# A fused state-space, attention and mixture-of-experts kernel: text rows are prepared earlier, logits go between other products, expert tiles are loaded sooner, and TensorE is given unread work

## The chip, the cores and the metric

The kernel runs on one core of a Trainium2 chip. The metric is device time of one execution in microseconds (us). Three runs of the kernel before took 2265.6, 2267.47 and 2272.73 us, so the median is 2267.47 us.

## What is computed

Eight sequences of 768 rows of 256 numbers go through three stages (float32 throughout):

```
K = 2.0 * einsum('chn,hnl->chl', C*B, exp(log_dA * arange(256))).real      # 256 image rows a batch
h = concatenate([K, txt], axis=1)                                          # + 512 text rows
q, k, v = layernorm(h) @ Wq, @ Wk, @ Wv          # 16 query heads, 4 key heads, 64 wide; q, k rotated
h = h + softmax(q k^T / 8) v @ Wo
logits = layernorm(h) @ Wr + br                  # 8 experts, the best 2 of each row, softmax of those 2
h = h + sum over the 2 of gate * (relu(x @ W1[e] + b1[e]) @ W2[e] + b2[e])
```

The image rows come from `x` (8, 256, 64, 2), the text rows from `txt` (8, 512, 256). The output is (8, 768, 256).

## The kernel before, in words

The program is three blocks of instructions with a barrier between them. In a block each engine works through its own list and meets the others at semaphores.

`vandermonde` makes the powers of the state-space model on VectorE, multiplies them on TensorE, and stores the image rows of batch 0 in `img_d`. The rows of the other seven batches stay in the tile `kt`, and are stored at the start of the next block.

`attention` works in 32 iterations (8 batches by 4 key heads) of 24 steps. A step is one tile of 128 queries of one head against 768 keys: TensorE makes the scores in two banks of PSUM (L656), VectorE the row maximum (L812), ScalarE the exponential (L725), VectorE a transpose (L818), and TensorE multiplies by the values (L663). Ahead of the first step stands a start that is not overlapped with any step. SyncE loads batch 0 into `a_x` (`load(0)`, L516 and L517). VectorE takes the statistics of its 6 tiles (`stats`, L496 to L504 and `refine`, L485 to L488) and normalises four of them (L850), GpSimd the other two (L781). TensorE transposes them (jobs "n" of the list `FIRST`, L633), projects keys, the queries of group 0 and of group 1 (L642), ScalarE copies each result out (`evacuate`), VectorE rotates keys and queries of group 0 in four calls of `rotate` (L470 to L475), in scratch that lies in `a_probT`, which shares its memory with `kt`. Then SyncE moves the keys and, with 16 DMAs, the queries (L622), and TensorE starts the first scores. Each projected job needs one of four banks, and the list waits on `x_out` (results copied out) for it.

`route` and `experts` stand in the third block. `route` takes 8 batches, of 6 tiles each: TensorE multiplies the attention rows by `Wo` (`project`, L980, 8 matmuls a tile), VectorE adds the residual and normalises. Of the batch before, TensorE transposes after tile 1 (`turn`, L988), makes the logits after tile 2 (`logits`, L996, 12 matmuls on 8 columns), and counts after tile 3 (`counts`, L1003 and L1004). VectorE chooses the experts (`choose`, L1110 to L1125) and the slots (`place`), and GpSimd scatters the rows to `xs_d`, where each expert has a range of slots (L963). When all are placed, `tile_table` makes on VectorE, for each of 103 tiles of 128 slots, its expert and its first slot (L1190 to L1212), and 128 empty rows ("pads") are written behind each expert's last row (L934, L1066).

`experts` takes the 103 tiles one after the other. SyncE loads the rows (`load`, L1258) and W1 of the expert (`load_w1`, L1262) into a ring of 4, TensorE transposes (L1292), multiplies by W1 (`up`, L1302) and by W2 (`down`, L1309), VectorE adds the bias and multiplies by the gate (L1382, L1384), GpSimd adds the rows to the output by an indirect DMA (L1365). Before SyncE's first row load stands a wait for all that was scattered, the pads and the stored residual (`landed`). GpSimd's add of a tile waits for the adds of the tiles two and three before it; where the expert changes it also waits for the tile just before (the value is in `adds_i`). Tiles beyond the last filled one ("spare" tiles) repeat the last filled tile with a gate of zero, and each of them counts as such a change.

## Time and profile before

| what | value |
|---|---|
| median of 3 runs | 2267.47 us |
| profiled execution, its own time | 2265.04 us |
| its span, first to last instruction | 2263.3 us |
| VectorE busy, 1000 to 1575 us (attention) | 556.40 of 575.00 us |
| TensorE busy, 1700 to 1800 us (route) | 100.00 of 100.00 us |
| TensorE busy, 2000 to 2200 us (experts) | 200.00 of 200.00 us |
| mean granted clock of TensorE | 0.959 |

All times of rows are counted from the span's start. Between the span and the time of the same execution lie 1.74 us. The granted clock is TensorE's share of full speed, and it has two levels here, 1.00 (2.4 GHz) and 0.50 (1.2 GHz). A matmul of float32 stands in the trace as two records, so that 8 matmuls read x16; transposes have one record each.

### The profile page before, as it was taken

To read this page: it belongs to the slowest core of one execution; us is meant where nothing else is said; L and a number is where in the kernel's file an instruction comes from. 1 tells how busy PE (TensorE), PEld (TensorE's weight loads), DVE (VectorE), ACT (ScalarE), POOL (GpSimd) and SP (SyncE) were. 2 spreads that over 40 slices of the span, in tenths; PEclk is the share of its full clock that TensorE was granted. 3 is DMA by queue.
4 is the path that set the end of the run, shared out by engine and by line. 5 is a ranking of instruction groups with operands and counts; after the bars stand their busy time and mean duration, and the time that the engine had idled before them with its cause. 6 is when DMAs were issued, how large, how long until landed. Compare 5 with 4: busy or idle time off the path is not lost. (4 is left out here: it accounts for less than half of the span.)

```text
span 2263.3 us, 59177 instructions
## 1 busy us (share of the span) xinstructions
PE 2047.4 (90%) x21098; PEld 1237.6 (55%) x21099; DVE 1770.0 (78%) x3212; ACT 1072.6 (47%) x2463; POOL 879.4 (39%) x833
## 2 busy tenths in 40 slices
PE   0369999999999999999999999997899949999997
PEld 0234444444444444444444445443588839999996
DVE  8769999999999999999999999999144544444443
ACT  2035655655556555655665565555021114444442
POOL 0023454264344542642444436221034443444443
PEclk6689999999999999999999999999899969999998
DMA  2143543634544445435444453453677648898885
GB/s 51 43 107 90 136 118 92 159 106 103 142 113 126 117 107 137 116 108 128 120 120 120 102 133 105 117 131 95 202 258 269 216 136 212 210 212 209 215 210 117
DMA packets 189542, 317.28 MB, mean 140 GB/s; under 512 B 48661, under 2 KB 127121, under 8 KB 189329
## 3 DMA queue, kind: packets, MB, share of 16 engines
q1 hardware_dynamic: 156640, 275.39, 45.1%
q0 software_dynamic: 19440, 25.83, 6.2%
q10 hardware_dynamic: 13248, 13.13, 1.7%
q8 instruction: 144, 2.36, 0.5%
q14 instruction: 70, 0.57, 0.1%
HBM read 214.75 MB, written 92.31 MB: 136 GB/s over the span
## 5 line engine op out<-in xcount | busy, mean ns | idle before, releaser
L725 ACT ACTIVATE a_prob<-ps_s,a_nmax 128x768 f32<-128x768 f32 x768 | 686.3, 898 | 578.9 <-DVE a_nmax L812 578.9
L812 DVE TENSOR_REDUCE a_nmax<-ps_s 128x1 f32<-128x768 f32 x768 | 694.1, 943 | 49.4 <-PE ps_s L656 44.2
L818 DVE STREAM_TRANSPOSE a_probT<-a_prob 128x768 f32<-128x768 f32 x768 | 700.0, 949 | 1.4 <-PE ps_o L663 1.4
L656 PE MATMUL ps_s<-a_kT,a_qT 64*128 64x384 f32 x3072 | 614.7, 514 | 54.7 <-ACT a_prob L725 50.8
L663 PE MATMUL ps_o<-a_probT,a_vrep 32*64 32x384 f32 x12288 | 561.2, 491 | 6.8 <-DVE a_probT L818 5.0
L656 PEld LDWEIGHTS ps_s<-a_kT,a_qT 64*128 64x128 f32 x3072 | 259.7, 186 | 391.5 <-ACT a_prob L725 275.3
L788 POOL TENSOR_TENSOR a_o<-a_o,a_invrow 128x1536 f32<-128x1536 f32 x32 | 110.0, 3437 | 791.0 <-ACT a_o L733 791.0
L663 PEld LDWEIGHTS ps_o<-a_probT,a_vrep 32*64 32x64 f32 x12288 | 243.6, 132 | 293.8 <-issue 129.9
L470 POOL TENSOR_TENSOR a_prod<-a_raw,a_table 128x384 f32<-128x384 f32 x304 | 294.5, 1002 | 29.1 <-DVE a_qp L475 22.1
L1365 POOL DMA_INDIRECT out_dram<-e_y,e_row_i x103 | 160.6, 1559 | 239.9 <-DMA out_dram<-e_y,e_row_i 138.6
L1302 PE MATMUL ps_r<-e_xT,e_w 128*128 128x128 f32 x1648 | 201.8, 276 | 0.0
L1309 PE MATMUL ps_r<-ew,e_hT 128*128 x824 | 194.7, 379 | 0.0
L1302 PEld LDWEIGHTS ps_r<-e_xT,e_w 128*128 128x128 f32 x1648 | 193.3, 193 | 0.1
L1340 ACT ACTIVATE e_hT<-ps_r,e_b_now 128x128 f32<-128x128 f32 x412 | 117.8, 368 | 158.9 <-PE ps_r L1302 100.0
L980 PE MATMUL ps_r<-wo,r_oT 128*128 128x256 f32 x768 | 180.9, 397 | 9.7 <-POOL base L945 9.7
L642 PE MATMUL ps_o<-a_xT,wq 128*128 128x384 f32 x512 | 185.8, 501 | 0.0
L980 PEld LDWEIGHTS ps_r<-wo,r_oT 128*128 128x128 f32 x768 | 151.5, 200 | 32.2 <-POOL base L945 10.4
L1309 PEld LDWEIGHTS ps_r<-ew,e_hT 128*128 128x128 f32 x824 | 148.8, 190 | 16.0
L963 POOL DMA_INDIRECT xs_d<-r_xn,r_idx x96 | 93.8, 977 | 150.1 <-DVE h L1078 119.1
L725 ACT ACTIVATION_READ_ACCUMULATOR a_prob<-ps_s,a_nmax 128x1 f32 x768 | 151.0, 197 | 0.0
L642 PEld LDWEIGHTS ps_o<-a_xT,wq 128*128 128x128 f32 x512 | 91.0, 189 | 88.9 <-issue 25.6
L1382 DVE TENSOR_TENSOR e_y<-ps_r,eb 128x256 f32<-128x256 f32 x103 | 43.7, 424 | 99.9 <-PE ps_r L1309 97.9
(211 smaller groups left out, 1291.5 us busy)
## 6 DMA issues: line engine op xcount, KB each, us to landing
e_w<-in_L_ffn_W_dram SPq DMA_DIRECT2D x103, 512.0 KB, 4.3
a_qT<-q_d SPq DMA_DIRECT2D x124, 384.0 KB, 8.9
a_vrep<-v_d SPq DMA_DIRECT2D x128, 192.0 KB, 3.8
a_invrow<-inv_d SPq DMA_DIRECT2D x64, 384.0 KB, 5.1
oT_d<-a_o SPq DMA_DIRECT2D x32, 768.0 KB, 3.3
r_oT<-oT_d SPq DMA_DIRECT2D x64, 384.0 KB, 8.4
q_d<-a_qp SPq DMA_DIRECT2D x31, 768.0 KB, 3.7
e_x<-xs_d SPq DMA_DIRECT2D x103, 132.0 KB, 3.6
```

Of the source, the lines that this page charges most:

```text
L470: eng.tensor_tensor(scratch[n], a, f, ALU.mult).then_inc(done, 1)
L642: last = pe.matmul(X[:, 0:HALF], w, xn[:, k, HALF * c:HALF * c + HALF], start=(k == 0), stop=(k == KC - 1))
L656: last = pe.matmul(S[:, s % 2, r, 0:HALF], qT[rows, par, 2 * hp + c, P * t:P * t + P], kT[rows, par, :], start=True, stop=True)
L663: last = pe.matmul(O[DH * c:DH * c + DH, q, 0:HALF], vrep[rows, j % NQ, j // NQ, :], keys(par, c, j, rows), start=(j == 0), stop=(j == NJ ...
L725: act.activation(prob[:, s % RING, :].rearrange("p (r k) -> p r k", r=2), S[:, s % 2, :, 0:HALF], ACT.Exp, bias=nmax[:, s % RING:s % RING ...
L812: v.tensor_reduce(nmax[:, s % RING:s % RING + 1], S[:, s % 2, :, 0:HALF], AX.XY, ALU.max, negate=True).then_inc(max_ready, 1)
L818: v.transpose(turned(par, s), prob[:, s % RING, :]).then_inc(t_ready, 1)
L980: last = pe.matmul(A[:, t % 3, 0:D], oT[:, q, c // 2, c % 2, P * t:P * t + P], wo[:, c, :], start=(c == 0), stop=(c == KV * 2 - 1))
L1302: last = pe.matmul(H[:, q, P * f:P * f + P], w1[:, n, c, P * f:P * f + P], xT[:, q, P * c:P * c + P], start=(c == 0), stop=(c == KC - 1))
L1309: last = pe.matmul(Y[:, q, 0:D], hT[:, q, P * c:P * c + P], w2[:, bass.ds(ex, 1), c, :], start=(c == 0), stop=(c == FC - 1))
L1340: last = act.activation(hT[:, q, P * f:P * f + P], H[:, q, P * f:P * f + P], ACT.Relu, bias=b1_now[:, n, f:f + 1], scale=1.0)
L1365: pool.indirect_dma_start(out=acc_d, out_offset=bass.IndirectOffsetOnAxis(ap=row_i[:, n:n + 1], axis=0), in_=y[:, n, :], in_offset=None, c ...
```

## The change

At the start of attention:
- The text rows of batch 0 are loaded and normalised in the first block, with `normalise_rows` on VectorE. The buffers for it are allocated before both blocks. Only the two image tiles are left for the second block, all on VectorE.
- The list `FIRST` begins with the text transposes (8), the keys of tokens 384 to 767, the image transposes (4), then the other keys, and the queries in the same order of halves.
- `rotate` of these works in `a_prod`, and the wait for `rows_stored` stands behind the four calls. Keys are moved by halves.
- Ahead of the first scores TensorE makes 16 matmuls of the identity by `wv`, 256 columns each, into a bank that nobody reads. They wait until the first job of group 1's queries is copied out.

In the routing:
- the 12 logit matmuls stand in pairs behind the last six of the eight matmuls of tile 2, no longer behind all eight.
- TensorE's first product waits no longer for GpSimd's constants; the counts do.

In the experts:
- SyncE waits no longer for all that was scattered before the first loads. For tiles 0 to 7 it reads from a small table (`needs_i`) whether the rows of the first seven batches fill the tile (`placed` 1) or not (`placed` 2); later tiles wait for `placed` 2. W1 is loaded in turn with the rows. The wait for the stored residual moved to GpSimd.
- A spare tile takes expert 7 and the pads behind its last row. The row numbers in the pads lie beyond the output, so that the add leaves them out, and it no longer counts as a change of expert. The table has some steps fewer.

```diff
+AHEAD = 8
@@ vandermonde
+                sp.dma_start(x0[:, IT:TT, :], io["txt"][0].rearrange("(t p) d -> p t d", p=P)).then_inc(x_in, 16)
...
+                v.wait_ge(x_in, 16)
+                normalise_rows(v, Tally(v, text_dve), x0, ln, range(IT, TT)).then_inc(text_ready, 1)
@@ attention
-    FIRST = N_JOBS + K_JOBS + Q_JOBS + Q_JOBS
+    FIRST = [("text", 0, 0), ("text", 1, 0), ("k", 1, 0), ("k", 1, 1), ("image", 0, 0), ("k", 0, 0), ("k", 0, 1),
+             ("q", 1, 0), ("q", 1, 1), ("q", 0, 0), ("q", 0, 1)] + Q_JOBS
@@ attention, sync
-                hold(sp, part["k"], 2 * LINKS)
-                move_k(0, 0)
+                for r in (1, 0):
+                    hold(sp, part["k"], (2 - r) * LINKS)
...
@@ attention, tensor
-                pe.wait_ge(norm_ready, 1)
-                pe.wait_ge(norm_first, 1)
+                pe.wait_ge(text_ready, 1)
...
+                    if n == IMAGE_AT:
+                        pe.wait_ge(norm_ready, 1)
...
-                pe.wait_ge(x_out, FIRST_AT["q1"])
+                pe.wait_ge(x_out, len(FIRST) - NQ + 1)
+                for _ in range(16):
+                    pe.matmul(O[:, len(FIRST) % NQ, 0:D], ident[:], wv[:, 0, 0:D], start=True, stop=True)
@@ attention, vector
-                v.wait_ge(rows_stored, (NB - 1) * 16)
-                flat = probT[:].rearrange("p a b q -> p (a b q)")
-                for job in "kq":
-                    for c in range(2):
-                        rotate(v, job, c, c, [flat[:, HALF * n:HALF * n + HALF] for n in range(4)], FIRST_AT[job] + 2 * c + 2, [])
+                for job, c, number in (("k", 1, 0), ("k", 0, 1), ("q", 1, 0), ("q", 0, 1)):
+                    rotate(v, job, c, number, [prod[:, n, :] for n in range(4)], FIRST.index((job, c, 1)) + 1, [])
+                v.wait_ge(rows_stored, (NB - 1) * 16)
@@ route, gpsimd
+            if isinstance(b, int) and b >= NB - 2:
+                if b == NB - 1:
+                    for r in range(2):
+                        pool.wait_ge(zeroed[r], 16 * (NE // 2))
+                pool.nop().then_inc(placed, 1)
@@ route, tensor
                 last = pe.matmul(A[:, t % 3, 0:D], oT[:, q, c // 2, c % 2, P * t:P * t + P], wo[:, c, :], start=(c == 0), stop=(c == KV * 2 - 1))
+                if beside is not None and c >= KV * 2 - TT:
+                    logits(beside, [c - (KV * 2 - TT)])
...
-        pe.wait_ge(const, 4)
@@ route, vector
+            k.link(v.tensor_scalar(full[:], off[:, 0, 0:1], 1.0 / P, -1.0, ALU.mult, ALU.add))
+            k.link(v.tensor_scalar(needs_i[:], tile_no[:, 0:AHEAD], full[:], 1.0, ALU.is_gt, ALU.add))
@@ tile_table
-    link(v.tensor_scalar(jr[:], j[:], last[:], None, ALU.min))
...
-    link(v.tensor_scalar(ind[:], j[:], last[:], None, ALU.is_gt))
...
+    v.tensor_scalar(src_i[:], start[:], run[:, NE - 1:NE], None, ALU.min).then_inc(rows_ready, 1)
...
-    link(v.tensor_tensor(turn[:, 1:NT], turn[:, 1:NT], ind[:, 1:NT], ALU.max))
@@ experts, sync
         def load(j, n):
+            if isinstance(j, int) and j < AHEAD:
+                needs = sp.value_load(at(needs_i, j), min_val=1, max_val=2)
+                hold(sp, placed, needs)
...
-        for n in range(2):
-            load_w1(n, n)
-        for s, value in landed:
-            sp.wait_ge(s, value)
         for n in range(RING):
             load(n, n)
-        for n in range(2, RING):
             load_w1(n, n)
@@ experts, gpsimd
+        pool.wait_ge(h_stored, 16 * NB)
```

What the change moves is seen in each engine's list of instructions. First TensorE's list at the start of attention, the kernel before (`a_x` holds the normalised rows, `wk` the key weights; the waits are in brackets):

```order
L633 MATMUL ps_o<-ident,a_x 128x128 [waits loaded,a_norm_first,a_norm_ready]
L633 MATMUL ps_o<-ident,a_x 128x128 x11
L642 MATMUL ps_o<-a_xT,wk 128x384 [waits a_x_out]
L642 MATMUL ps_o<-a_xT,wk 128x384
L642 MATMUL ps_o<-a_xT,wk 128x384 [waits a_x_out]
L642 MATMUL ps_o<-a_xT,wk 128x384
```

The same place in the changed kernel:

```order
L663 MATMUL ps_o<-ident,a_x 128x128 [waits loaded,a_text_ready]
L663 MATMUL ps_o<-ident,a_x 128x128 x7
L679 MATMUL ps_o<-a_xT,wk 128x384 [waits a_x_out]
L679 MATMUL ps_o<-a_xT,wk 128x384 x3
L666 MATMUL ps_o<-ident,a_x 128x128 [waits a_x_out,a_norm_ready]
L666 MATMUL ps_o<-ident,a_x 128x128 x3
L679 MATMUL ps_o<-a_xT,wk 128x384 [waits a_x_out]
L679 MATMUL ps_o<-a_xT,wk 128x384
```

The wait for the image's normalisation (`a_norm_ready`) now stands behind eight text transposes and four key matmuls.

Second, TensorE's list of one batch of the routing, the kernel before (`wo` is the output projection, `wr` the router, `r_xT` the transposed rows of the batch before):

```order
L980 MATMUL ps_r<-wo,r_oT 128x256 [waits r_h1_ready]
L980 MATMUL ps_r<-wo,r_oT 128x256 x7
L992 ISA
L996 MATMUL ps_r<-wr,r_xT 128x8 [waits r_mask_ready,r_xT_ready]
L996 MATMUL ps_r<-wr,r_xT 128x8 x11
```

And in the changed kernel:

```order
L1025 MATMUL ps_r<-wo,r_oT 128x256 [waits r_h1_ready]
L1025 MATMUL ps_r<-wo,r_oT 128x256 x2
L1040 ISA
L1044 MATMUL ps_r<-wr,r_xT 128x8 [waits r_mask_ready,r_xT_ready]
L1044 MATMUL ps_r<-wr,r_xT 128x8
L1025 MATMUL ps_r<-wo,r_oT 128x256
L1044 MATMUL ps_r<-wr,r_xT 128x8 x2
L1025 MATMUL ps_r<-wo,r_oT 128x256
L1044 MATMUL ps_r<-wr,r_xT 128x8 x2
```

The number of matmuls is the same; the logits moved into the product of tile 2, and their wait for `r_xT_ready` with them.

Third, SyncE's list at the start of the experts, the kernel before (`exp_i` and `src_i` are the expert and the first slot of each tile, read into a register before the DMA that uses them):

```order
L1254 UNCONDITIONAL_BRANCH [waits r_table_ready]
L1261 TENSOR_LOAD exp_i
L1261 ISA x2
L1262 ISA
L1262 DMA e_w<-in_L_ffn_W_dram 128x2x512
L1261 TENSOR_LOAD exp_i
L1261 ISA x2
L1262 ISA
L1262 DMA e_w<-in_L_ffn_W_dram 128x2x512
L1257 TENSOR_LOAD src_i [waits r_scattered0,r_h_stored,r_scattered1,r_zeroed1,r_zeroed0]
L1257 ISA x2
```

And in the changed kernel:

```order
L1300 UNCONDITIONAL_BRANCH [waits r_table_ready]
L1304 TENSOR_LOAD needs_i
L1304 ISA x2
L1306 TENSOR_LOAD src_i [waits r_placed]
L1306 ISA x2
L1307 ISA
L1307 DMA e_x<-xs_d 128x264
L1310 TENSOR_LOAD exp_i
L1310 ISA x2
L1311 ISA
L1311 DMA e_w<-in_L_ffn_W_dram 128x2x512
```

The wait for everything scattered became a wait for `r_placed`, one more register is read for each of the first rows, and rows and weights come in turn.

## Rows read from the trace of the kernel before

**Rows 1.** Busy time by engine, attention: stretch, length, then PE, PEld, DVE, ACT, POOL busy, clock.

```profile
155.00:500.00 345.00, 326.63 (x3642) 152.93 (x3642) 335.27 (x425) 202.62 (x443) 150.31 (x157) 1.00 0.47 118
```

**Rows 2.** Timeline, start of attention: start us, length us, engine, line, operation, [idle before <-releaser].

```profile
104.54 0.38 SPq L516 DMA_DIRECT2D a_x<-img_d  x1
...
106.02 11.77 SPq L614 DMA_DIRECT2D img_d<-kt  x7
108.94 2.06 DVE L496 BATCH_NORM_STATS2 a_st<-a_x 128x6 f32<-128x256 f32 x6 [15.88 <-DMA a_x<-in_txt_dram]
...
117.50 2.82 PE L633 MATMUL ps_o<-ident,a_x 128*128 128x128 f32 x12 [17.04 <-POOL a_x L781]
...
121.01 8.28 PE L642 MATMUL ps_o<-a_xT,wk 128*128 128x384 f32 x16 [0.69 <-ACT a_xT L713]
...
127.15 1.96 DVE L470 TENSOR_TENSOR a_probT<-a_raw,a_table 128x384 f32<-128x384 f32 x4 [10.75 <-ACT a_raw L719]
...
129.12 10.48 PE L642 MATMUL ps_o<-a_xT,wq 128*128 128x384 f32 x32
...
139.43 10.97 SPq L622 DMA_DIRECT2D a_qT<-a_qp  x16
...
143.54 2.66 PE L656 MATMUL ps_s<-a_kT,a_qT 64*128 64x384 f32 x8 [3.94 <-DMA a_qT<-a_qp]
...
152.68 1.78 DVE L812 TENSOR_REDUCE a_nmax<-ps_s 128x1 f32<-128x768 f32 x2
...
156.12 1.78 DVE L812 TENSOR_REDUCE a_nmax<-ps_s 128x1 f32<-128x768 f32 x2
```

**Rows 3.** DMA issues, 104 to 107 us: count, KB each, median us to landing.

```profile
a_x<-img_d SPq DMA_DIRECT2D x1, 256.0 KB, 2.7
```

**Rows 4.** Busy time by engine around the first scores (columns as in Rows 1).

```profile
140.00:150.00 10.00, 5.59 (x16) 2.22 (x16) 2.87 (x3) 2.54 (x6) 3.34 (x4) 0.69 0.57 135
...
160.00:170.00 10.00, 5.05 (x24) 1.84 (x24) 10.00 (x13) 5.62 (x12) 0.06 (x1) 1.00 0.75 197
```

**Rows 5.** Chain of waits, routing and first expert tiles: start us, length us, what.

```profile
1645.61 2.58 PE ps_r L996 x24
1648.19 5.24 PE ps_r L980 x16
...
1675.03 3.56 PE ps_r L980 x16
...
1865.31 1.79 PE ps_r L1302 x16
1867.10 1.73 PE ps_r L1309 x8
```

**Rows 6.** TensorE in a stretch behind logits: busy, granted clock, DMA share, GB/s.

```profile
1649.20:1652.40 3.20, 3.20 (x9) 0.50 0.81 238
```

**Rows 7.** Timeline of the routing, the batch at 1669 to 1681 us.

```profile
1677.51 0.21 DVE L1124 TENSOR_TENSOR r_mask<-r_hot 128x48 f32<-128x48 f32 x1
...
1678.42 0.32 PE L1003 MATMUL ps_r<-r_mask,r_below 128*128 128x48 f32 x2
```

**Rows 8.** Timeline, end of the routing and start of the experts.

```profile
1847.53 0.26 DVE L1209 SCALAR_TENSOR_TENSOR src_i<-t_e,t_start 128x103 int32<-128x103 f32 x1
...
1848.73 1.74 SPq L1262 DMA_DIRECT2D e_w<-in_L_ffn_W_dram  x2
...
1858.49 3.66 SPq L1258 DMA_DIRECT2D e_x<-xs_d  x4
...
1862.18 2.91 PE L1302 MATMUL ps_r<-e_xT,e_w 128*128 128x128 f32 x16
```

**Rows 9.** The tile of W1, 1846 to 1880 us: its DMAs.

```profile
DMA to landing us min/median/max: 3.8/4.2/4.8
```

**Rows 10.** Timeline of the end.

```profile
2248.16 0.35 DVE L1384 TENSOR_SCALAR e_y<-e_y,e_gate 128x256 f32<-128x256 f32 x1
...
2255.17 1.55 POOL L1365 DMA_INDIRECT out_dram<-e_y,e_row_i  x1 [2.98 <-DMA out_dram<-e_y,e_row_i]
```

More of the change, by code:

```diff
@@ L627, in project @@
                 def project(X, job, c, h, xn, g):
-                    if job == "n":
+                    if job == "text":
+                        for m in range(TT - IT):
+                            last = pe.transpose(X[:, P * m:P * m + P], x[:, IT + m, P * c:P * c + P], ident[:])
+                    elif job == "image":
+                        for m in range(4):
+                            last = pe.transpose(X[:, P * m:P * m + P], x[:, m % IT, P * (m // IT):P * (m // IT) + P], ident[:])
+                    elif job == "n":
                         for m in range(4):
@@ L1007, in iteration @@
             for t in range(TT):
-                project(b, q, t)
+                project(b, q, t, b - 1 if not first(b) and t == LOGITS_AT else None)
                 if not first(b) and t == TURN_AT:
                     turn(b - 1, 1 - q)
-                if not first(b) and t == LOGITS_AT:
-                    logits(b - 1)
                 if not first(b) and t == COUNTS_AT:
@@ L1172, in _ @@
         loop(iteration, drain, v)
-    return [(zeroed[q], 16 * (NE // 2)) for q in range(2)] + [(h_stored, 16 * NB)] + [(scattered[q], NB // 2 * TT * TOPK * 16) for q in range(2)]
+    return placed, h_stored
 def tile_table(v, sb, dve, run, base, j, pairs, exp_i, src_i, held_by, adds_i, rows_ready):
@@ L1184, in tile_table @@
     ni = sb("t_ni", [P, NE], I32)
-    last = sb("t_last", [P, 1])
-    jr, e, start, ind, turn = (sb(f"t_{x}", [P, NT]) for x in ("jr", "e", "start", "ind", "turn"))
+    e, start, turn = (sb(f"t_{x}", [P, NT]) for x in ("e", "start", "turn"))
     past = sb("t_past", [P, NT, NE - 1])
@@ L1279, in tile @@
                 load_w1(j + RING, n)
+            if isinstance(j, int) and j == AHEAD - RING - 1:
+                sp.wait_ge(placed, 2)
         loop(sp, tile)
```

124 lines of the change are left out of this document (78 added, 46 removed).

## The prediction

> **What bounds the kernel now.** I read the busy time by engine in long stretches first, then the chain of waits, then the timeline where the chain leaves one engine. In attention VectorE is busy 335.27 of 345 us [rows 1], so every step waits for it, and an earlier first step moves the whole stage forward. Its start is not overlapped: loading, normalising, projecting and rotating pass the work from engine to engine until 143.54 us [rows 2]. Then the chain stays on TensorE through the products of the routing, leaves it for the last batch's choosing, placing and scattering, comes back at 1862 us [rows 8], and stays with 1.79 + 1.73 us of products a tile [rows 5]. At the end it hangs on the last adds of GpSimd [rows 10]. So four places count: the start of attention, TensorE's clock in the routing, the start of the experts, the last adds. Time taken away at each goes fully through, since the stages between are bound by VectorE or TensorE throughout.
>
> **The start of attention.** The second block starts at 104.5 us [rows 2], for the image rows need the first block's last results. Before, VectorE started its statistics at 108.94 us, behind the text load, with six tiles (2.06 us) [rows 2]. Now the text was handled in the first block, where VectorE idles 15.88 us before that row; four tiles take 4/6 of 2.06, the 15 small steps some 3, four normalisations 1.6, together about 6.5 us, which fits. Left are two image tiles: the load lands after 2.7 us [rows 3], at 107.3; statistics, small steps and two normalisations take about 5 us; the image is ready at 112.2, where before TensorE had to wait until 117.50 [rows 2].
>
> Meanwhile TensorE transposes text and makes the keys of the second half. At the slow clock one transpose takes 2.82/12 = 0.24 us and one job of 4 records about 2.6 us (8.28 us for 16 records held both clocks, and 10.48/8 = 1.31 us is the price of a job at the full one) [rows 2]. Eight transposes, a copy and two jobs end at 112.3. So both are there together, TensorE has worked almost without a pause, and I take the full clock from about 114 us. Then image transposes and copy to 114.0, two key jobs to 116.6, copy 0.5. A call of rotate takes (139.43 - 127.15)/4 = 3.07 us [rows 2]; keys of the second half are rotated while this goes on, and the other three calls end at 117.2 + 9.2 = 126.4. At the slow clock the two key jobs take 2.6 us more: 129.0. Before, the last call ended at 139.4, where the 16 query DMAs start [rows 2]. SyncE's seven stores of image rows are issued by 117.8 (106.02 + 11.77) [rows 2], before it is needed. From the first query DMA to the first scores went 143.54 - 139.43 = 4.1 us [rows 2], so scores could begin at 130.6.
>
> But the unread matmuls stand ahead of them in TensorE's list. They wait for the first job of group 1 to be copied, which waits for the last rotation: about 127.2. They are 32 records of 256 columns, as those of the product in the routing, of which 16 take 3.5 us at the full clock (3.56 with the start of the counts [rows 5]); so 7.0 us, to 134.2. Scores start there, 9.3 us earlier than before. What they buy is the clock: before, TensorE stood idle for 3.94 us ahead of 143.54 [rows 2], and in 140 to 150 us the granted clock was 0.69 [rows 4]. From the first scores to the row maximum at which VectorE's regular pace of 3.44 us a pair begins (156.12 - 152.68) went 9.14 us. At the full clock this is between 6.9 (two pairs at that pace) and 9.14; I take 7.6, 1.5 less. The start gives 9.3 + 1.5 = 10.8 less 0.4 for the chance of the slow clock: **10.4 us**, between 7 and 12.5.
>
> **The routing.** The product behind the logits should take 3.5 us. It takes 5.24 in five of seven batches (all have such a row; 1648.19 stands for five, 1675.03 with 3.56 for two) [rows 5], since the clock fell, to 0.50 in 1649.2 to 1652.4 [rows 6]. Just before the falls TensorE had 24 records of 8 columns. Now there are 256-column records between these. Attention holds a clock of 1.00 with TensorE busy 5.05 of 10 us [rows 4], and here half of the time streams 256 columns; I take it that no fall is left: 5 x 1.73 = 8.7 us. The logit records themselves take 2.58/24 = 0.107 us each, which is the time of a weight load more than that of 8 columns. One load in a run hides behind a wide record, and the next wide record shows its own: 24 in a run cost 24 x 0.107, and so do six runs of four. No gain or loss there.
>
> The choosing starts later: the last product of tile 2 and the logits now end together, and VectorE does the addition and statistics of that tile first, 0.7 to 0.8 us. Before, in the batch at full clock, the mask was there at 1677.72 (1677.51 + 0.21) and TensorE came for it at 1678.42 [rows 7], 0.7 us later. So the wait is 0 to 0.3 us a batch, 1 us in all. The wait on GpSimd's constants held TensorE at the start of the block for some 0.75 us. The routing gives 8.7 - 1.0 + 0.7 = **8.4 us**, between 4 and 11 (how many falls the kernel before has depends on where they meet the logits).
>
> By the Trainium skill, "TensorE: Matmul & The Clock Gate", section "Step-by-step: what each phase is for", TensorE pulls weight loads ahead of running matmuls, so that the next tile's weights load during this one. If it pulled two of each run behind the wide record instead of one, the change would hide 6 x 7 x 0.107 = 4.5 us more. The chain shows 0.107 us for every one of 24 in a run and cannot tell; it is a rival below.
>
> **The start of the experts.** Before, the table was written at 1847.79 (1847.53 + 0.26), W1 of two tiles issued from 1848.73, the rows of the first tile at 1858.49 when all was scattered, and `up` of tile 0 began at 1862.18 [rows 8]. Is the first tile full after seven batches? The reference's router on its own inputs sends 2616 of the first seven batches' rows to expert 0, 20.4 tiles, so all eight tiles need only `placed` 1, long there. The table loses about six steps and gains four (two of them ahead of it): 0.8 us earlier, 1847.0. One register read with its DMA takes 3.66/4 = 0.9 to 1.1 us [rows 8], the further register 0.5. Rows of tile 0 go at 1848.4, W1 at 1849.6, tile 1's W1 at 1852.4, and so on every 2.8 us, faster than the 3.7 us of a tile. W1 lands after 3.8 to 4.8 us [rows 9]: `up` of tile 0 at about 1853.9, 8.3 us earlier. It begins at the slow clock, as before (2.91 us for 16 records [rows 8] where 1.79 is the full price [rows 5]), perhaps longer: minus 0.8. **7.5 us**, between 4 (W1 landing late beside the last scatters) and 9. The scatters go on until 1857.7, before the adds need GpSimd (tile 0 would be ready at about 1861.7) and before tile 8 is loaded.
>
> **The last adds.** The last result is ready at 2248.51 (2248.16 + 0.35), the last add starts at 2255.17, for the four spare tiles go in single file: each issues for 1.55 us and the next waits 2.98 more for it to land, 4.53 us apart [rows 10]. (The router fills 99 tiles of 103.) Without the order they are bound by their results, 3.7 us apart, and GpSimd's own 1.56 us: tile 101 starts at 2248.0, tile 102 at 2249.8. That is 5.4 us; adds that leave all rows out may be quicker or not (0 to 1.5 us), or their order may still bind somewhere (then 3). **5.4 us**, between 3 and 7.
>
> **Sum.** 10.4 + 8.4 + 7.5 + 5.4 = 31.7 us. The profiled execution took 2265.04, 1.74 above its span and 2.43 under the median of the three runs. By it 2233.3, by the median 2235.8. I say 2236 us. The ends of the four terms (18 and 39.5 us) seldom come together; its own range is 2229 to 2244.
>
> **Rivals.**
> - *The unread matmuls run at the slow clock or the full clock comes late.* They take 14 us instead of 7 and the first scores wait for them. For it: TensorE lost the clock behind 3.94 us without work [rows 2, 4]. Against: its own jobs end within a microsecond of the moment at which the matmuls may start. Time: 7.0 + 1.5 lost, 2244.
> - *The experts don't start earlier*, because W1 lands late behind scatters, or because rows and weights come in turn and tile 0's W1 was loaded ahead before. For it: before, both waits ended together only because the rows came last. Then 7.5 is lost: 2243.
> - *The weight loads of the logits hide* (the rule above): 2231.5. The clock row cannot exclude it.
> - *Slower: the mixed stretch lowers the clock.* Each logit pair leaves the array nearly idle for 0.43 us beside 0.43 us of columns. If this drops the clock in every batch, and it stays down for long, each microsecond at 0.50 costs half a microsecond. The gains elsewhere are 23.3 us, and the clock costs 8.7 now in five falls; it turns slower once TensorE spends over 64 us of the routing at 0.50 (2 x 32), 9 in each of seven batches, where it was 3.4. At 12 us a batch: 7 x 6 = 42 - 8.7 = 33 us more than before, 2277. Against: 1.00 in attention at 5.05 of 10 us busy [rows 4]. One fall in each batch, as in five of them now, is a milder form: then only the 8.7 is not gained, and up to 3.5 more is lost, 2245 to 2248.
> - *The change doesn't do what it says*: the rotated keys might still wait for the stores of image rows, through the queue of SyncE; these are issued by 117.8 us and nothing is due before. That would cost 1 to 3 us.
>
> **Chances.** The forecast 60%; one of the first two rivals 17%; hidden loads 9%; milder clock 10%; slower 2%; other 2%. The range of 8 in 10 is 2228 to 2247. A difference under 0.3% (6.8 us) is about what a measurement of this kernel can't tell from none. Faster than that 0.96, same 0.02, slower 0.02.
>
> **What would show it.** In the profile after: VectorE's statistics of text before 100 us; the query DMAs at 126 to 129; unread matmuls with about 0.22 us a record, and first scores right behind them at 134 to 137, with a clock of 1.00; a product behind the logits of 3.5 us in all seven batches, and the counts not waiting over 0.3 us for the mask; `up` of tile 0 about 17 us after the last batch's counts, not 26; the last add within 1.5 us of the last result. The forecast is wrong if the clock falls in the mixed stretch, if `up` of tile 0 starts with the last scatter, or if the steps of attention don't keep the lead of the start.

## The result, and the profile after

The changed kernel took 2259.99 us (median of 11 runs, 2251.3 to 2267.8) against 2266.44 us of the kernel before in the same comparison (11 runs): a ratio of 0.9968, 95% interval 0.9956 to 0.998. Forecast were 2236 us. Its own profiled execution took 2259.99 us, with a span of 2258.2. (One execution of e15 below, of 2481.78 us at a mean granted clock of 0.83, was in a slower state, and is left out of that run's range and ratio.)

The start of attention and the last adds came out as forecast. TensorE and VectorE at the start of attention, in the changed kernel's timeline (columns as in [rows 2]):

```profile
103.12 0.39 SPq L639 DMA_DIRECT2D a_x<-img_d  x1
105.82 0.75 DVE L80 BATCH_NORM_STATS2 a_st<-a_x 128x6 f32<-128x256 f32 x2 [6.72 <-DMA a_x<-img_d]
...
125.64 9.34 SPq L653 DMA_DIRECT2D a_qT<-a_qp  x13
...
126.21 7.17 PE L742 MATMUL ps_o<-wv,ident 128*128 128x256 f32 x32
133.31 1.56 PE L693 MATMUL ps_s<-a_kT,a_qT 64*128 64x384 f32 x8
...
140.89 1.78 DVE L854 TENSOR_REDUCE a_nmax<-ps_s 128x1 f32<-128x768 f32 x2
...
1599.06 0.77 PE L1025 MATMUL ps_r<-wo,r_oT 128*128 128x256 f32 x1 [9.04 <-DVEq L1216]
```

First scores stand at 133.31 (before 143.54 [rows 2]), the pair of row maxima that was at 152.68 [rows 2] at 140.89, 11.8 us sooner. Between the two lie 7.58 us (140.89 - 133.31), where 7.6 were forecast and 9.14 stood before. The first product of the routing stands at 1599.06, where before it was 1610.97: 11.9 us sooner. At the end the last result is ready at 2249.04 and the last add starts 1.28 us later, not 6.66 [rows 10]:

```profile
2248.69 0.35 DVE L1431 TENSOR_SCALAR e_y<-e_y,e_gate 128x256 f32<-128x256 f32 x1
2250.32 1.55 POOL L1411 DMA_INDIRECT out_dram<-e_y,e_row_i  x1 [0.30 <-issue]
```

The lead of 11.9 us is gone at the end of the routing. From the start of its first product to the start of its last record it took 223.6 us where the kernel before took 207.1. TensorE's waits in the stretch 1590 to 1840 us have one entry that has grown, from 0.7 us once in the kernel before (us in total, times, longest):

```profile
PE ps_r L1044 <- ACT r_xT L1081: 11.3, 5, 3.8
```

L1044 is the first logit, L1081 ScalarE's copy of the turned rows ("turned" is transposed, in three thirds, each copied by itself). Batches are counted by the turned one, from 1; each is turned beside the products of the next. The five waits are those of batches 2 to 6. The timeline of batch 3:

```profile
1688.67 1.47 PE L1035 MATMUL ps_r<-ident,r_xn 128*128 128x128 f32 x12
1689.98 1.46 PE L1025 MATMUL ps_r<-wo,r_oT 128*128 128x256 f32 x6
1691.53 0.60 ACT L1081 ACTIVATE r_xT<-ps_r 128x512 f32<-128x512 f32 x1 [7.30 <-PE ps_r L1035]
1691.58 0.42 DVE L1125 TENSOR_TENSOR h<-ps_r,h 128x256 f32 x1 [3.92 <-remote]
...
1692.02 0.59 ACT L1081 ACTIVATE r_xT<-ps_r 128x512 f32<-128x512 f32 x1
1692.50 0.60 ACT L1081 ACTIVATE r_xT<-ps_r 128x512 f32<-128x512 f32 x1
...
1693.15 0.61 PE L1044 MATMUL ps_r<-wr,r_xT 128*128 128x8 f32 x4 [1.71 <-ACT r_xT L1081]
```

VectorE at 1691.58 adds the product of tile 1, which ended before the turning began at 1688.67. ScalarE at 1691.53 copies the first third of the turning, which was done some 0.6 us after 1688.67. Both wake within 0.05 us of each other, over 2 us late, and the second and third copy follow without a pause, so their signals had all come. Two engines that wait for different work of TensorE wake together: TensorE's signals came late, not the copies. I call this late signals below.

The trace also keeps the time of each semaphore update, and says the same directly. The update for the product of tile 1 stands at 1691.44, those for the three thirds of the turning at 1691.50, 1691.56 and 1691.62, though the turning began at 1688.67. On time they come 0.61, 1.05 and 1.49 us behind its start (batches 1 to 7 of the kernel before).

Batches 4 to 6 look like batch 3, with the first copy 2.89 to 3.26 us behind the start of the turning. Batch 2 does not: its three copies start at 1657.45, 1658.93 and 1660.38, each as its own update comes, and the last is 4.4 us late. TensorE's wait there is the longest, 3.8 us. In this trace updates of TensorE's matmuls come late only around the turnings of batches 2 to 6, and in no part of attention or of the experts.

### The profile page after: what moved, and what is told of

The parts are those of the page before. It is cut to its first block and busy times, and to the rows that moved or that the text cites. A ratio compares the mean times of both kernels' runs of the same rounds, so it can differ in the third digit from the quotient of the medians.

```text
span 2258.2 us, 59284 instructions
## 1 busy us (share of the span) xinstructions
PE 2059.7 (91%) x21130; PEld 1246.8 (55%) x21131; DVE 1772.2 (78%) x3227; ACT 1071.2 (47%) x2463; POOL 875.3 (39%) x831
## 5 line engine op out<-in xcount | busy, mean ns | idle before, releaser
L1025 PE MATMUL ps_r<-wo,r_oT 128*128 128x256 f32 x768 | 189.7, 400 | 9.0 <-DVEq L1216 9.0
```

The source lines that it names most:

```text
L1025: last = pe.matmul(A[:, t % 3, 0:D], oT[:, q, c // 2, c % 2, P * t:P * t + P], wo[:, c, :], start=(c == 0), stop=(c == KV * 2 - 1))
```

## Was it the change? The same kernel on other chips

The changed kernel, without an edit, was run three times more. The chips are numbered by the results; the one of the first comparison is not told.

| kernel | chip | median us (range, runs) | late copies in (of the one traced execution) |
|---|---|---|---|
| changed, first comparison | not told | 2259.99 (2251.3 to 2267.8, 11) | batches 2 to 6 |
| changed | 13 | 2251.85 (2250.99 to 2255.83, 5) | 3 batches |
| changed | 14 | 2258.75 (2248.42 to 2272.35, 12) | 6 batches |
| changed | 2 | **2234.16** (2233.1 to 2235.44, 4) | none |
| before | 0, 13, 5, 2, 14 | 2264.19, 2265.3, 2265.62, 2264.2, 2266.27 | |

On chip 2 the ratio is 0.9865 (0.985 to 0.988), and on chip 14 it is 0.9971 (0.9951 to 0.9992). The kernel before tells the two apart by 2 us, the changed one by 25. There, on chip 2, the same place reads:

```profile
1678.97 1.47 PE L1035 MATMUL ps_r<-ident,r_xn 128*128 128x128 f32 x12
1679.29 0.42 DVE L1125 TENSOR_TENSOR h<-ps_r,h 128x256 f32 x1 [1.16 <-PE ps_r L1025]
1679.61 1.57 ACT L1081 ACTIVATE r_xT<-ps_r 128x512 f32<-128x512 f32 x3 [5.08 <-PE ps_r L1035]
...
1680.28 1.46 PE L1025 MATMUL ps_r<-wo,r_oT 128*128 128x256 f32 x6
1681.58 0.51 PE L1044 MATMUL ps_r<-wr,r_xT 128*128 128x8 f32 x4
```

From turning to first logit it takes 2.61 us (1681.58 - 1678.97), and 4.48 in the rows of the first comparison (1693.15 - 1688.67).

What the late signals cost is more than the waits. Stretches of the whole routing, for the kernel before, the changed one in the first comparison, on chip 14 and on chip 2 (columns as in [rows 1]):

```profile
1611.00:1818.00 207.00, 207.00 (x1047) 183.73 (x1048) 95.53 (x514) 33.18 (x50) 72.71 (x81) 0.95 0.71 237
```

```profile
1599.00:1820.00 221.00, 209.60 (x1035) 184.85 (x1036) 94.64 (x514) 33.40 (x50) 71.45 (x83) 0.94 0.66 221
```

```profile
1597.30:1826.00 228.70, 219.44 (x1048) 192.36 (x1048) 95.14 (x514) 33.51 (x50) 73.50 (x86) 0.91 0.64 214
```

```profile
1599.00:1798.00 199.00, 199.00 (x1048) 177.73 (x1047) 95.52 (x514) 33.19 (x50) 72.92 (x84) 0.99 0.74 246
```

The undisturbed routing is 199 us at a clock of 0.99. In the first comparison TensorE stood idle for 221.00 - 209.60 = 11.4 us, and the clock of 0.94 is worth 221 x 0.06 = 13.3 us against 2.0: 11.3 more. 199 + 11.4 + 11.3 = 221.7, the row's 221.0. On chip 14 it is 9.3 of idle time and 228.7 x 0.09 - 2.0 = 18.6 of clock: 226.9 of 228.7. So a wait is followed, in some batches, by a stretch at half clock in which the mixed logits themselves run: in the first comparison behind the waits of 3.8, 2.1 and 2.0 us, and not behind the two of 1.7. The chain of waits of the changed kernel, first comparison, batch 2 (start, length, what):

```profile
1661.03 0.61 PE ps_r L1044 x4
1661.64 0.81 PE ps_r L1025 x2
1662.45 0.65 PE ps_r L1044 x4
1663.11 1.05 PE ps_r L1025 x2
1664.16 0.65 PE ps_r L1044 x4
```

A pair costs 0.65 + 1.05 = 1.70 us there, and 0.87 (six pairs 5.2 us) where the clock is 1.00. The times spread over 24 us on chip 14 and over 2.3 us on chip 2. That the number of such batches differs from execution to execution would account for this; it is not shown, since one execution of each kernel is traced.

## The experiments

All ratios are to runs of the kernel before on the same chip. The last column is read from one execution of each, which is not always a typical one: it took 2263.8 us in e8, the slowest of six, 2242.42 in e18, the slowest of four, and 2264.69 in e17.

| label | edit, to | chip | median us (range) | ratio (95%) | late copies |
|---|---|---|---|---|---|
| e1 | logits behind all eight, to changed | 0 | 2242.09 (2240.93 to 2245.4) | 0.9905 (0.989 to 0.992) | none |
| e2 | mix in tile 3, to changed | 0 | 2236.69 (2234.58 to 2236.8) | 0.9874 (0.9859 to 0.9889) | none |
| e3 | wait alone early, to changed | 0 | 2241.81 (2239.45 to 2243.07) | 0.9898 (0.9882 to 0.9913) | none |
| e4 | mix alone, to before | 0 | 2255.61 (2255.53 to 2258.78) | 0.9966 (0.9952 to 0.9979) | none |
| e5 | none | 13 | 2251.85 (2250.99 to 2255.83) | 0.9943 (0.993 to 0.9956) | 3 batches |
| e6 | no unread matmuls, to changed | 13 | 2251.15 (2249.17 to 2256.88) | 0.9944 (0.9931 to 0.9956) | 3 |
| e7 | 12 small matmuls ahead of routing | 13 | 2259.22 (2251.29 to 2266.45) | 0.997 (0.9958 to 0.9983) | 3 |
| e8 | wait on constants out of the loop | 13 | 2250.34 (2245.33 to 2263.8) | 0.9925 (0.9912 to 0.9938) | 4 |
| e9 | before + mix + start | 5 | 2243.43 (2241.14 to 2248.17) | 0.9913 (0.9899 to 0.9926) | none |
| e10 | before + mix + experts | 5 | 2246.0 (2244.09 to 2248.53) | 0.992 (0.9906 to 0.9933) | none |
| e11 | weights loaded first, to changed | 5 | 2233.83 (2232.51 to 2235.25) | 0.9862 (0.9847 to 0.9877) | none |
| e12 | e2 + other order on SyncE | 5 | 2235.38 (2233.91 to 2236.69) | 0.9873 (0.9858 to 0.9888) | none |
| e13 | none | 2 | 2234.16 (2233.1 to 2235.44) | 0.9865 (0.985 to 0.988) | none |
| e14 | as e9 | 2 | 2246.25 (2242.58 to 2247.79) | 0.9915 (0.9901 to 0.9929) | none |
| e15 | as e10 | 2 | 2246.38 (2243.93 to 2247.42) | 0.9914 (0.9901 to 0.9928) | none |
| e16 | as e2 | 2 | 2234.9 (2233.41 to 2236.25) | 0.9869 (0.9855 to 0.9884) | none |
| e17 | none | 14 | 2258.75 (2248.42 to 2272.35) | 0.9971 (0.9951 to 0.9992) | 6 |
| e18 | as e2 | 14 | **2240.44** (2240.14 to 2242.42) | 0.9885 (0.987 to 0.99) | 6 |

**First group (chip 0): which part of the edit loses?**

```diff
 # e1, in project()
-                if beside is not None and c >= KV * 2 - TT:
-                    logits(beside, [c - (KV * 2 - TT)])
             last.then_inc(oT_free, 1)
+            if beside is not None:
+                logits(beside, range(TT))
```

> The changed kernel with the logits put back behind all eight products of tile 2; everything else of the change stays. In the changed kernel TensorE waits about 5 us in five of the eight batches ahead of its first logit, and the routing stretch (first product 1599.06 to last product 1819.6) is 220.5 us long against 207.5 before. Theory A (TensorE comes to the wait on the copies of the turned rows after three products instead of eight, and its own finished products and turnings are then told late): the waits go, routing takes 206 to 208 us, the median is 2245 (2242 to 2248). Rival B (the mixed logits and products themselves keep the clock low and cost it): the same time, 2245, so this kernel does not tell A from B. Rival C (the loss comes from the earlier start of attention or from the transfers, which fall otherwise beside the routing): the waits stay, 2256 to 2262.

```diff
 # e2
-    TURN_AT, LOGITS_AT, COUNTS_AT = 1, 2, 3
+    TURN_AT, LOGITS_AT, COUNTS_AT = 1, 3, 4
```

> The changed kernel with the mixed logits in the products of tile 3 instead of tile 2, and the counts behind tile 4 instead of tile 3. TensorE then comes to the wait one whole product and more after its turnings, when the three copies have long been made. Theory A (the early wait): no wait over 1 us ahead of the first logit, routing 199 to 203 us, median 2236 to 2240, less than with the logits behind the products. Rival B (mixing itself): still about 5 us lost in most batches, 2255 to 2262. Rival C (transfers or the start): 2255 to 2262 too, with the wait at the same place.

```diff
 # e3: as e1, the two waits taken out of logits() and put into project()
+                if beside is not None and c == KV * 2 - TT:
+                    pe.wait_ge(xT_ready, beside * 3 + 3)
+                    pe.wait_ge(mask_ready, beside + 1)
```

> The changed kernel with the two waits ahead of the logits where they stand now, after three of the eight products of tile 2, but the logits themselves behind all eight products: the wait without the mixing. Theory A: the wait stays 4 to 6 us long in most batches of the loop and the median is 2256 to 2264. Rival B (mixing itself): no long wait, 2243 to 2248. Rival C: as the changed kernel, 2256 to 2262; it is told from A by the kernel with the logits behind the products.

e4 is the kernel before with the two parts of the change in `project` and `logits`, and nothing else.

> The kernel before with the mixed logits alone (after the last six of tile 2's eight products, the waits ahead of the first of them). Theory A and rival B: the routing is some 12 us longer than before, median 2276 to 2282. My prediction's sum for this edit alone: 8.7 us less, 2258. Rival C (the loss needs the rest of the change): 2258 to 2262.

e1 came out at 2242.1, e2 at 2236.7, as theory A had it. But e3, with the wait where the changed kernel has it, came out at 2241.8, and e4, with the mix, at 2255.6, 8.6 us under the kernel before on its chip. So neither the wait nor the mix loses by itself on this chip. Each theory missed: A e3 and e4, B e2 and e4 (and e3 by 1 us), C all four. I took it for an interaction with the rest of the change. What I did not see: the changed kernel had not run in this group, only elsewhere.

**Second group (chip 13): what in the program makes signals late?**

> The changed kernel once more, without an edit, for a second trace and a second spread of times beside the three bridging kernels. What has been seen: the mixed logits gain 8.6 us in the kernel before; in the changed kernel they lose (2260 with them against 2242 with the logits behind the products), and in its trace TensorE's signals of finished products and turnings come 2.6 to 3.1 us late in batches 2 to 6. Theory D (a standing property of this program: where its code or its waits lie): the signals are late again in the same batches, median 2255 to 2264, spread over 8 us wide. Rival E (a chance of one chip or one loading of the program): no late signals, median 2232 to 2238.

```diff
 # e6
-                for _ in range(16):
-                    pe.matmul(O[:, len(FIRST) % NQ, 0:D], ident[:], wv[:, 0, 0:D], start=True, stop=True)
```

> The changed kernel without the 16 unread matmuls ahead of the first scores; the mixed logits stay. Theory D1 (the code's place in TensorE's instruction stream decides over the late signals): the routing's code lies 16 matmuls earlier, the late signals go or move to other batches, median 2233 to 2240. Rival D2 (what runs beside it: the waits and transfers of the routing): they stay, 2255 to 2264. For the unread matmuls themselves: by the sum in the prediction they are worth little either way; the first scores come up to 3 us earlier at a lower clock, net within 2 us.

```diff
 # e7
+        for _ in range(12):
+            pe.matmul(L[:, 0:NE], ident[:], wr[:, 0, :], start=True, stop=True)
         pe.wait_ge(wo_in, 16)
```

> The changed kernel with 12 matmuls of 8 columns put ahead of the routing's first product, into a bank whose content the first logits replace; TensorE waits 9 us there anyway, so they cost nothing by themselves. Theory D1 (code's place): the late signals go or move, median 2233 to 2250, and the time differs from that of the changed kernel by more than 3 us. Rival D2: late signals in batches 2 to 6 as before this edit, 2255 to 2264.

```diff
 # e8
         def counts(b):
-            pe.wait_ge(const, 2)
 ...
+        pe.wait_ge(const, 2)
         pe.wait_ge(wo_in, 16)
```

> The changed kernel with TensorE's wait on the two constant tables taken out of the counts and put ahead of the routing, so that the loop's code on TensorE is word for word that of the kernel before with the mixed logits, which had no late signals. Theory D3 (one instruction more in the loop of the routing is what tips it): no late signals, median 2233 to 2240. Rivals D1 and D2: late signals or not by the code's place (the waits are one or two instructions), so as the changed kernel, 2255 to 2264.

All four have waits of TensorE for the copies: 5.0 us in 3, 5.7 in 3, 5.1 in 3, 7.3 in 4. No edit removed them, not even e8, whose loop code on TensorE is that of e4, so D3 fell. D1 had them go or move: they did not go, e6 came out at 2251.15 for its 2233 to 2240, and e7 at 2259.22 for its 2233 to 2250. That they stand in other batches (2, 5, 6 in e5; 3, 4, 6 in e6 and e7; 2, 3, 4, 6 in e8) says little, since the first comparison and chip 13 differ in this with one and the same kernel. D2 had 2255 to 2264 for these kernels, and theory D had the same for e5: of the four only e7 lies there. I took D2 for the nearest, which was not shown.

e6 tells of the unread matmuls: first scores at 128.98, where e5 has 133.38, and the clock in two stretches behind them 0.61 and 0.50, where e5 has 1.00 twice. e6:

```profile
128.00:138.00 10.00, 6.97 (x24) 2.92 (x24) 5.73 (x7) 3.86 (x8) 2.31 (x3) 0.61 0.61 144
138.00:148.00 10.00, 7.24 (x22) 2.70 (x20) 9.29 (x11) 5.50 (x11) 7.26 (x8) 0.50 0.44 153
```

e5:

```profile
128.00:138.00 10.00, 8.46 (x42) 5.75 (x40) 2.37 (x3) 1.88 (x4) 2.64 (x3) 1.00 0.58 138
138.00:148.00 10.00, 5.38 (x26) 1.84 (x24) 10.00 (x13) 5.63 (x12) 7.76 (x8) 1.00 0.42 129
```

So they do hold the clock up, as the prediction had it, and the first scores stand 4.4 us later for it. The routing's first product stood at 1596.84 in e6, 1601.27 in e5, and between 1597.3 and 1601.3 in all four traces of the unedited changed kernel: without them it is no slower, and perhaps some us faster. The medians (2251.15 and 2251.85) don't tell.

**Third group (chip 5): which half of the rest?** e9 has the functions up to `route` of the changed kernel and from `route` on those of e4; e10 the reverse.

> The kernel before with two parts of the change: the mixed logits in tile 2 and the new start of attention (with the unread matmuls); routing otherwise and experts are those of before. Late signals on TensorE have so far been seen in all five traces of kernels with the mixed logits in tile 2 beside all the rest of the change, and not in the trace of the mixed logits alone on the kernel before. Theory S (the rest that is needed is in the start of attention: the routing comes 12 us earlier and otherwise against its transfers): late signals in three or more batches, median 2255 to 2265. Rival X (it is in the part of the experts and the end of routing): none, median 2255.6 - 11 = 2243 to 2247.

> The kernel before with the mixed logits in tile 2 and the change's part in the routing's end and the experts (mask wait, rows awaited one by one, spare tiles that read pads), with the start of attention of before. Theory X (this part is what the late signals need besides the mixing): late signals in three or more batches, median 2255 to 2265. Rival S: none, and the parts add up: 2255.6 less about 4 at the start of the experts and 5 to 6 at the last adds, 2245 to 2248.

```diff
 # e11, SyncE in route: b1, w2, b2 of all eight experts behind the first rows, not one's a batch
-            sp.dma_start(w2[:, b], ...)
+            for x in range(NE) if b == 0 else ():
+                sp.dma_start(w2[:, x], ...)
```

> The changed kernel with the second layers' weights and biases of all eight experts loaded at once during the routing's first batches, instead of one expert's per batch. The late signals begin in batch 2 at the earliest and end with batch 6, where SyncE is also slow at issuing those loads (3 to 5 us each). Theory T (the transfers beside the turnings hold the signals back): late signals only in batches 1 to 3, if at all, median 2236 to 2250. Rival (something else in the program): late signals in batches 2 to 6 in any case, 2250 to 2264.

```diff
 # e12, to e2: SyncE's first loads of the experts
-        for n in range(RING):
-            load(n, n)
-            load_w1(n, n)
+        for f, n in ((load, 0), (load_w1, 0), (load, 1), (load, 2), (load_w1, 1), (load, 3), (load_w1, 2), (load_w1, 3)):
+            f(n, n)
```

> The kernel with the mixed logits in tile 3 (2236.7) and another order on SyncE at the start of the experts: rows 0, first layer 0, rows 1, rows 2, first layer 1, rows 3, first layers 2 and 3. In its trace the second tile's products wait for the turning of tile 2, whose rows are issued 6.7 us after those of tile 0, behind two first layers. Theory (the rows of tile 2 are what is late): they are issued 1.4 us sooner and the first layer of tile 1 as much later, which then decides; 1 us is won, 2235 to 2236.5. Rival (each register load on SyncE is the price and the order is worth nothing): 2236.5 to 2238.

None of the four had late signals, in e9 and e10 against both theories' need for one of them. e11 had none either, as theory T allowed (its time, 2233.83, is under T's 2236 to 2250), but a chip without late signals gives that whatever the edit. So e11 tests nothing. Only here did I lay the chips beside the results: every kernel with late signals had run on other chips than every kernel without.

In e12 the rows of tile 2 were issued 1.1 us sooner (5.32 us behind those of tile 0, and 6.41 in e2), and then the second tile waited for W1 instead: it landed at 1839.24, and the products start at 1839.28. From the last counts matmul to them it is 24.6 us, as in e2. The ratios are 0.9873 and 0.9874. So the rival was right in that the order won nothing; the time of 2235.38 alone, on another chip than e2, would have fallen to the theory.

**Fourth group (chip 2) and fifth (chip 14): the chip.**

> The changed kernel a third time, on one chip with the next three. Theory C (the combination of the mix in tile 2 and both halves of the rest makes the late signals, on any chip): late signals in three or more batches, 2250 to 2262. Rival K (the chip makes them): with late signals as in theory C on a chip that has them, and on one that has not, none and 2232 to 2239.

> The kernel before with the mixed logits in tile 2 and the new start of attention, a second time (2243.4 the first time, no late signals). Theory C: again 2241 to 2247, also where the changed kernel has late signals beside it. Rival K: 2255 to 2265 with late signals where the changed kernel has them.

> The kernel before with the mixed logits in tile 2 and the change's part in the experts, a second time (2246.0 the first time, no late signals). Theory C: again 2244 to 2249. Rival K: 2258 to 2268 with late signals where the changed kernel has them.

> The changed kernel with the mixed logits in tile 3, a second time (2236.7 the first time, no late signals). Theory C, and rival K where the chip needs the mix in tile 2 as well: 2234 to 2240. If the chip makes signals late whatever the place of the mix: over 2245, or, since here TensorE does not stand at the wait when they come, 2236 to 2242 with late copies by ScalarE in the trace.

e13 had none and took 2234.16 us, within 2 us of the forecast. Theory C fell, rival K was met. e14 to e16 came out where both had them on a chip without late signals, and so tell nothing between the two. Chip 14 then had late signals, with the tile 3 kernel beside:

> The changed kernel on a further chip. Rival K of before, now the theory (late signals come with the chip or the occasion): either 2233 to 2237 without late signals or 2250 to 2262 with them in three or more batches; nothing between.

> The changed kernel with the mixed logits in tile 3, on the same chip. If the changed kernel has late signals there: 2234 to 2242 if only a wait right behind the turnings pays for late signals, 2248 to 2262 if they cost it wherever the mix stands. If it has none: 2234 to 2238.

Both came out in the ranges that were set down for late signals (2250 to 2262, and 2234 to 2242 if only a wait right behind the turnings pays). No time of e18 reaches the lowest of e17 (2242.42 and 2248.42). e18 is what tells late signals from their price. Its timeline on chip 14, batch 3:

```profile
1680.35 1.47 PE L1035 MATMUL ps_r<-ident,r_xn 128*128 128x128 f32 x12
1681.65 4.91 PE L1025 MATMUL ps_r<-wo,r_oT 128*128 128x256 f32 x22
1683.34 0.60 ACT L1081 ACTIVATE r_xT<-ps_r 128x512 f32<-128x512 f32 x1 [7.44 <-PE ps_r L1035]
1683.40 0.42 DVE L1125 TENSOR_TENSOR h<-ps_r,h 128x256 f32 x1 [3.97 <-remote]
...
1684.31 0.60 ACT L1081 ACTIVATE r_xT<-ps_r 128x512 f32<-128x512 f32 x1
...
1686.41 0.51 PE L1044 MATMUL ps_r<-wr,r_xT 128*128 128x8 f32 x4
```

The signals are as late as in the changed kernel (ScalarE's first copy 2.99 us behind the start of the turning, 2.86 in the first comparison, 0.64 on chip 2), though the mix is a tile away. But the first logit comes at 1686.41, 6.06 us behind the turning, and finds its rows copied since 1684.91. TensorE's wait for the copies is 0.5 us in total in 1640 to 1800 us, for 7.2 of the changed kernel on the same chip, the routing takes 199.9 us for 228.3, and the time is 2240.4 for 2258.75. The mix in tile 2 brought the first logit to 2.61 us behind the turning. The copies on time are done after 2.20 (1679.61 + 1.57 - 1678.97): a slack of 0.4 us, enough on chips 0, 5 and 2, and 1.5 to 2.1 us too little in most of the late batches.

e18 still took 5.5 us more than the same kernel on chip 2 (e16, 2234.9). In the traces, little of that lies in the routing (199.9 us, 199.1 in e16). Behind it the last batch's logits, which nothing covers, have a late signal too: VectorE reads them at 1818.04, 6.15 us after the last logit matmul has ended (0.04 us in e16), and 12.51 us behind the start of the last turning (8.84 in e16). The mix in tile 3 does nothing for this one.

Whether the kernel before has late signals on such a chip is not shown: the only trace of it, on a chip that is not told, has none, and its time hardly moves. It makes its first logit 4.76 us behind the turning (1672.29 - 1667.53). Late copies are done 4.43 to 4.84 us behind it in batches 3 to 6 of the first comparison, but after 6.51 in batch 2, and after 4.57 to 6.65 in e18. So its cover would take up most of the lateness, not all of it.

## Why the prediction was wrong

In the first comparison the gain was 6.5 us (2266.44 - 2259.99), and 31.7 were forecast. On a chip without late signals the forecast was near: 2234.16 us for 2236. The terms, from the traces of the kernel before and of e13:

| term | forecast | e13 | how |
|---|---|---|---|
| start of attention, with the start wait | 10.4 + 0.7 | 12.4 | 1610.97 - 1598.59, first product |
| routing, rest | 7.7 | 8.1 | its end 1818.48 and 1798.05, less the 12.4 |
| start of the experts | 7.5 | 5.4 | counts of the last batch to products of the second tile, 29.4 and 24.0 |
| last adds | 5.4 | 5.6 | last product by W2 to the end, 16.2 and 10.6 |
| sum | 31.7 | 31.5 | spans 2263.3 - 2231.9 = 31.4 |

That the sums agree within 0.2 us is partly luck: the start gave 1.3 us more than forecast, the routing 0.4, the last adds 0.2, and the experts 2.1 less. The wait on GpSimd's constants was to give 0.7 us, and TensorE's wait ahead of the routing's first product went from 9.7 us to 9.0.

**The step that failed** is in "The routing": "The choosing starts later", the one place where it counted waits of the moved logits. It weighed what waits behind the logits (the mask, 1 us) and left out what they wait for: the wait for the copies of the turned rows stands in its sum at nothing. Both waits of `logits` moved forward with it, from behind eight products to behind three: 2.2 us less of cover behind the turning. The prediction gave that cover no number and no price if it is gone. With late signals the price was 11.4 us of waits and 11.3 of clock in the first comparison, in place of a gain of 8.4. e17 and e18 show it on one chip: with the mix in tile 2 and in tile 3 the routing takes 228.3 and 199.9 us, though both have late signals in six batches. The rows of before do not show late signals; that the margin shrinks from 2.6 us to 0.4 was there to read.

**The clock.** The mix does hold it: e4 alone gains 8.6 us on before (forecast 8.7 for the falls less 1.0 for the mask; TensorE's waits for the mask are 0.4 us in e13). The rival "the mixed stretch lowers the clock" is false by this and by 0.99 in the routing on chip 2. The first comparison's time, 2259.99 us, lies in its span of 2245 to 2277, by another mechanism: an idle TensorE ahead of the mix, with a fall in three of seven batches.

**Hidden weight loads.** A pair costs 0.34 + 0.53 = 0.87 us in the chain on chip 2, which is 4 x 0.107 + 2 x 0.22: none of the four loads is saved beyond the one that the sum had. By the Trainium skill, "TensorE: Matmul & The Clock Gate", section "Step-by-step: what each phase is for", weight loads are pulled ahead of running matmuls; this trace shows one of a run hidden, not two.

**The start of the experts** was mis-sized by 2. `up` of tile 0 comes 20.5 us behind the counts in e13 (1815.38 to 1835.90). The prediction's list of signs has 17, but its own times give 18.1 (1853.9 less the counts of before at 1835.77). It let `up` of tile 0 wait for its own W1 alone. In e13, TensorE's counts, SyncE's loads, the turning of tile 1, and the products of tiles 0 and 1:

```profile
1815.38 0.63 PE L1053 MATMUL ps_r<-r_mask,r_below 128*128 128x48 f32 x2 [2.79 <-issue]
...
1828.56 0.37 SPq L1307 DMA_DIRECT2D e_x<-xs_d  x1
1830.03 0.41 SPq L1311 DMA_DIRECT2D e_w<-in_L_ffn_W_dram  x1
...
1831.81 0.34 SPq L1307 DMA_DIRECT2D e_x<-xs_d  x1
1833.23 0.38 SPq L1311 DMA_DIRECT2D e_w<-in_L_ffn_W_dram  x1
1835.03 0.33 SPq L1307 DMA_DIRECT2D e_x<-xs_d  x1
1835.42 0.69 PE L1338 MATMUL ps_r<-ident,e_x 128*128 128x128 f32 x2 [3.91 <-DMA e_x<-xs_d]
...
1835.90 3.15 PE L1348 MATMUL ps_r<-e_xT,e_w 128*128 128x128 f32 x16
...
1839.34 1.95 PE L1348 MATMUL ps_r<-e_xT,e_w 128*128 128x128 f32 x16
```

The turning of tile 1 stands ahead of `up` of tile 0 in TensorE's list. Its rows are issued at 1831.81, behind W1 of tile 0, and land 3.57 us later, at 1835.38. W1 of tile 0 had landed at 1833.98, so the rows of tile 1 decide, by 1.4 us. SyncE is slower than forecast too: from one tile's rows to the next are 3.25 us, not 2.8, 1.78 of them from W1 to the next rows, with their further register. In e13 the rows of tile 2 land at 1839.02, just as `up` of tile 0 ends, so they cost the second tile nearly nothing. Before, the four loads of rows were issued within 3.66 us [rows 8]. An order with the rows of tile 1 ahead of W1 of tile 0 was not tried (e12 left that pair as it was).

**The range** came from the spread of costs that rows showed, and the runs of before (2265.6 to 2272.73) gave no hint that one program can differ by 25 us between chips. With late signals even its 8-in-10 range of 2228 to 2247 is missed.

What stays open: what makes TensorE's signals late by up to 4.5 us in the loop (a chip, or the occasion, since each chip was used once; every execution on record was profiled, so the profiler's own part is not known either), and why it begins only in batch 2 or later. Taking away the unread matmuls, moving the code and moving the wait on constants did not remove it (e6 to e8). The transfers beside the routing are untested, since e11 met no late signals to remove. The tile 3 kernel with e11's order was not tried, nor the logits behind all eight products (e1) on a chip with late signals.

## What to carry to other kernels

A wait that is moved forward must be priced by the slack it leaves: read in the trace how long before it its signal comes, and keep a few us where the partner's answer (here turning, copy, logits) crosses two engines. One tile later, with a slack of 3.85 us (6.06 - 2.21) instead of 0.4, gave the same time where the signals were on time (2234.9 and 2234.16 on chip 2) and lost 5.5 us instead of 25 where they were late. And run the kernel in question beside its experiments on the same chip: two groups were spent on an interaction that was a difference of chips or occasions, since the kernel before was equal on all and so seemed to vouch for them.

## What the runs showed of the hardware

- TensorE's signals of finished matmuls can reach VectorE and ScalarE together and late, on three of six occasions here, in up to six batches of one execution, while TensorE's own work goes on. The first copy behind a turning then started mostly 2.6 to 3.9 us behind its start, for 0.64 on time, and the last signal of a turning came up to 4.5 us late. The kernel before moves by no more than 2.3 us over all of them.
- A wait of TensorE can cost more than its length. In the first comparison the granted clock was 0.50 in 1662 to 1672 us, behind the wait of 3.8 us, and again for 7 us behind each of those of 2.1 and 2.0; waits of 11.4 us came with 11.3 us lost to the clock. On chip 14 it was 9.3 us with 18.6.
- With 16 unread matmuls ahead of a stage its clock was 1.00 from 128 to 148 us, and without them 0.61 and 0.50.
